# Perceiver attention scores: float32 keys and queries as 32-row tiles four abreast, in place of three products of rounded parts

## The reference, cut to what matters

```python
q = _qdq(x) @ _qdq(wq).T + bq
kv = cond @ wkv.T + bkv
k, v = jnp.split(kv, 2, axis=-1)          # 16 heads of width 16, 1601 keys
attn = jax.nn.softmax(jnp.einsum('bnhd,bmhd->bhnm', q, k) * scale, axis=-1)
o = jnp.einsum('bhnm,bmhd->bnhd', attn, v).reshape(B, N, C)
```

## Time and profile before

| | |
|---|---|
| median of 3 runs | 2300.67 us (2297.53 to 2301.21) |
| span of the profiled execution, first to last instruction | 2296.0 us |
| the rest of the median, outside of the span | 4.7 us |
| scores of the first strip, of the last | 33.4 us, 1759.8 us |
| TensorE matmul busy, mean granted clock | 2102.5 us (92%), 0.973 |
| VectorE busy, ScalarE busy, GpSimd busy | 1751.3 us (76%), 1441.0 us (63%), 684.0 us (30%) |

### The profile page before, as it was taken

How to read it: one execution, slowest core, us unless ns; L and a number is a source line. 1 busy time by engine, 2 the same in 40 slices (tenths; PEclk the granted TensorE clock), 3 DMA queues, 4 the chain that set the end, 5 groups by cost and what they waited for, 6 DMA issues and landing times. The chain is left out here.

```text
span 2296.0 us, 56054 instructions
## 1 busy us (share of the span) xinstructions
PE 2102.5 (92%) x21448; PEld 1456.2 (63%) x21448; DVE 1751.3 (76%) x3728; ACT 1441.0 (63%) x3012; POOL 684.0 (30%) x646
## 2 busy tenths in 40 slices
PE   7999999999999999999999999999997149999975
PEld 5666666666666666666666666666664037777754
DVE  5557887979797978888888888797978736656646
ACT  2667676768676767676777767676867124444433
POOL 1002040404131322213130404040403427767770
PEclk9999999999999999999999999999999569999998
DMA  7586672323132313232323323232310136676648
GB/s 226 192 288 210 235 250 75 114 82 89 72 89 72 93 70 91 77 83 79 100 88 82 97 64 105 55 105 68 107 47 25 56 119 212 199 229 209 201 138 331
DMA packets 132711, 294.16 MB, mean 128 GB/s; under 512 B 21899, under 2 KB 89143, under 8 KB 126304
## 3 DMA queue, kind: packets, MB, share of 16 engines
q1 hardware_dynamic: 114016, 255.89, 35.7%
q0 software_dynamic: 18432, 34.69, 4.3%
HBM read 165.40 MB, written 108.27 MB: 119 GB/s over the span
## 5 line engine op out<-in xcount | busy, mean ns | idle before, releaser
L801 ACT ACTIVATE sb_probs<-S,sb_negmax 128x1604 f32<-128x1604 f32 x256 | 409.2, 1598 | 278.5 <-DVE sb_negmax L979 277.0
L793 ACT ACTIVATE sb_probsT<-W 128x384 f32<-128x384 f32 (+1 forms) x1024 | 473.6, 513 | 68.2 <-PE W L639 65.3
L639 PE MATMUL W<-sb_ident,sb_probs 128*128 128x128 f32 (+1 forms) x3328 | 478.3, 280 | 15.7 <-DVE sb_o_tok L992 8.0
L979 DVE TENSOR_REDUCE sb_negmax<-S 128x1 f32<-128x1604 f32 x256 | 466.2, 1821 | 2.9 <-PE S L629 1.2
L639 PEld LDWEIGHTS W<-sb_ident,sb_probs 128*128 128x128 f32 (+1 forms) x3328 | 363.5, 139 | 133.9 <-issue 64.7
L612 PE MATMUL W<-sb_wkv_in,sb_ctx 128*128 128x256 f32 (+1 forms) x1664 | 410.7, 389 | 14.2 <-ACT sb_probsT L793 6.6
L602 PE MATMUL W<-sb_ctx,sb_wkv_in 128*32 128x401 f32 x4096 | 399.3, 504 | 4.4 <-DVE sb_V L973 2.9
L612 PEld LDWEIGHTS W<-sb_wkv_in,sb_ctx 128*128 128x128 f32 (+1 forms) x1664 | 293.3, 187 | 79.1 <-ACT sb_probsT L793 25.7
L1335 POOL DMA_INDIRECT y_scratch<-sb_ys,sb_places x256 | 264.4, 1033 | 112.1 <-issue 109.0
L963 DVE SCALAR_TENSOR_TENSOR sb_K_lo<-W,sb_pair_cols,sb_K_hi 128x401 fp32r<-128x401 f32 x256 | 162.2, 633 | 175.5 <-ACT sb_K_hi L785 175.2
L785 ACT ACTIVATE sb_K_hi<-W,sb_pair_cols 128x401 fp32r<-128x401 f32 x256 | 153.2, 598 | 181.5 <-PE W L602 181.4
(11 more groups left out here) (188 smaller groups left out, 2921.0 us busy)
## 6 DMA issues: line engine op xcount, KB each, us to landing
sb_ctx<-ctxT SPq DMA_DIRECT2D x32, 1604.0 KB, 7.7
xe_scratch<-sb_none SPq DMA_DIRECT2D x32, 1088.0 KB, 12.7
sb_xg<-xe_scratch SPq DMA_DIRECT2D x64, 544.0 KB
sb_BC<-bc_scratch SPq DMA_DIRECT2D x32, 1024.0 KB, 5.9
sb_Q_hi<-sb_q_hi SPq DMA_DIRECT2D x128, 128.0 KB, 4.5
sb_Q_lo<-sb_q_lo SPq DMA_DIRECT2D x128, 128.0 KB, 5.4
y_scratch<-sb_none SPq DMA_DIRECT2D x16, 1024.0 KB, 12.0
sb_rows<-y_scratch SPq DMA_DIRECT2D x16, 1024.0 KB, 8.1
```

What stands on the lines that cost most here:

```text
L639: ins = pe.transpose(W[0:keys_in(t), at * P:(at + 1) * P], probs[n % 2][:, t * P:t * P + keys_in(t)], ident[:])
L793: act.activation(probsT[k][n % (k + 1)][:, 0:wide], ring[bank_of("T", G, k)][:, 0:wide], ACT.Copy)\
L801: act.activation(probs[n % 2][:].rearrange("p (c k) -> p c k", c=QUADS), scores_of, ACT.Exp, bias=negmax[:, slot:slot + 1], accum_out=den[ ...
L979: dve.tensor_reduce(negmax[:, slot:slot + 1], scores_of, AX.XY, ALU.max, negate=True).then_inc(max_done, 1)
```

## The change

Keys and queries stay whole, in float32. ScalarE writes the keys once (`K`) and releases their bank; `k_low` is gone, and with it `K_lo`, `K_hi` and the semaphore between ScalarE and VectorE. GpSimd only places the queries (`q_own`), without the two further operations, and SyncE deals them with four DMAs for each half pair in place of eight. The scores are one product: four float32 matmuls, each on its own 32 rows of the array and into its own PSUM bank, in place of twelve matmuls of float32r.

```diff
 def freed_by(job):
-    return "act" if job[0] == "T" else "dve"
+    return "act" if job[0] in ("T", "K") else "dve"
...
-        K_hi, K_lo = (sb(f"K_{m}", [P, STRIPS, CK + 1], F32R) for m in ("hi", "lo"))
+        K = sb("K", [P, STRIPS, CK])
...
-        q_hi, q_lo = (sb(f"q_{m}", [P, STEPS, 2, N], F32R) for m in ("hi", "lo"))
-        Q_hi, Q_lo = ([sb(f"Q_{m}{n}", [P, STRIPS, 2, 2, N], F32R) for n in range(2)] for m in ("hi", "lo"))
+        Q = [sb(f"Q{n}", [P, STRIPS, 2, 2, N]) for n in range(2)]
...
-                for part, whole in ((q_hi, Q_hi), (q_lo, Q_lo)):
-                    for c in range(QUADS):
-                        sp.dma_start(whole[half][32 * c:32 * c + 32, :, :, :, :].rearrange("p s g h n -> p s (g h n)").bitcast(F32),
-                                     part[:, 2 * half:2 * half + 2, :, :].rearrange("p g h n -> p (g h n)").bitcast(F32)).then_inc(q_in[half], 16)
+                for c in range(QUADS):
+                    sp.dma_start(Q[half][32 * c:32 * c + 32, :, :, :, :].rearrange("p s g h n -> p s (g h n)"),
+                                 q_own[:, 2 * half:2 * half + 2, :, :].rearrange("p g h n -> p (g h n)")).then_inc(q_in[half], 16)
...
-                pool.tensor_tensor(q_own[:], *of_heads, ALU.mult).then_inc(q_own_up, 1)
-                pool.tensor_tensor(q_hi[:], *of_heads, ALU.mult).then_inc(q_hi_up, 1)
-                pool.wait_ge(q_own_up, i + 1)
-                pool.wait_ge(q_hi_up, i + 1)
-                pool.tensor_tensor(q_lo[:], q_own[:], q_hi[:].bitcast(F32), ALU.subtract).then_inc(q_up, 1)
+                pool.tensor_tensor(q_own[:], *of_heads, ALU.mult).then_inc(q_up, 1)
...
-                pe.wait_ge(ring_free["dve"], free_at("K", n))
+                pe.wait_ge(ring_free["act"], free_at("K", n))
...
-                products = ((Q_hi, K_hi), (Q_hi, K_lo), (Q_lo, K_hi))
-                for n, (q, k) in enumerate(products):
-                    for c in range(QUADS):
-                        rows = slice(32 * c, 32 * c + 32)
-                        cn = CK + 1 if c == 0 else CK - 1
-                        ins = pe.matmul(S[:, 512 * c:512 * c + cn], q[half][rows, s, g, :, :].rearrange("p h n -> p (h n)"),
-                                        k[rows, s, 0:cn], start=(n == 0), stop=(n == len(products) - 1))
+                for c in range(QUADS):
+                    rows = slice(32 * c, 32 * c + 32)
+                    cn = CK if c == 0 else CK - 1
+                    ins = pe.matmul(S[:, 512 * c:512 * c + cn], Q[half][rows, s, g, :, :].rearrange("p h n -> p (h n)"),
+                                    K[rows, s, 0:cn], start=True, stop=True)
...
-                act.activation(K_hi[:, s, 0:CK], ring[bank_of("K", n)][:, 0:CK], ACT.Identity,
-                               bias=pair_cols[:, g * STRIPS + s:g * STRIPS + s + 1]).then_inc(k_hi_up, 1)
+                act.activation(K[:, s, :], ring[bank_of("K", n)][:, 0:CK], ACT.Identity,
+                               bias=pair_cols[:, g * STRIPS + s:g * STRIPS + s + 1]).then_inc(ring_free["act"], 1)
...
-            def k_low(n):
-
-                _, g, s = step_of(n)
-                dve.wait_ge(k_hi_up, n + 1)
-                dve.scalar_tensor_tensor(K_lo[:, s, 0:CK], bank("K", n)[:, 0:CK],
-                                         pair_cols[:, g * STRIPS + s:g * STRIPS + s + 1],
-                                         K_hi[:, s, 0:CK].bitcast(F32), ALU.add, ALU.subtract).then_inc(ring_free["dve"], 1)
...
-                if G + STRIPS < ALL_STRIPS:
-                    k_low(G + STRIPS)
```

More of the change, by code:

```diff
@@ L321, in mixer_phase @@
         ring_free = {"act": sem("ring_free_act"), "dve": sem("ring_free_dve")}
-        k_hi_up = sem("k_hi_up")
         var_up = sem("var_up")
@@ L326, in mixer_phase @@
         q_f_up = sem("q_f_up")
-        q_own_up = sem("q_own_up")
-        q_hi_up = sem("q_hi_up")
         q_up = sem("q_up")
@@ L462, in _ @@
             pool.memset(neg_half[:], -0.5).then_inc(consts, 1)
-            for part in (K_hi, K_lo):
-                pool.memset(part[:, :, CK:CK + 1].bitcast(F32), 0.0).then_inc(consts, 1)
             pool.iota(iota_e[:], [[1, E]], base=0, channel_multiplier=0,
@@ L470, in _ @@
                       allow_small_or_imprecise_dtypes=True).then_inc(consts, 1)
-            pool.wait_ge(consts, 9)
+            pool.wait_ge(consts, 7)
             pool.affine_select(out=ident[:], in_=ident[:], compare_op=ALU.not_equal, fill=1.0, base=0,
@@ L478, in _ @@
                                pattern=[[1, P]], channel_multiplier=-1).then_inc(consts, 1)
-            pool.wait_ge(consts, 12)
+            pool.wait_ge(consts, 10)
             pool.affine_select(out=headmask[:], in_=headmask[:], compare_op=ALU.is_ge, fill=0.0, base=DH * STRIPS - 1,
                                pattern=[[DH * STRIPS, 2]], channel_multiplier=-1).then_inc(consts, 1)
-            pool.wait_ge(consts, 13)
+            pool.wait_ge(consts, 11)
             def rstd_q(i):
@@ L493, in part_q @@
                 for half in range(2):
-                    after(pool, q_in[half], 16 * 2 * QUADS * i)
+                    after(pool, q_in[half], 16 * QUADS * i)
                 of_heads = (q_f[:].rearrange("p b g n -> p (b g) n").unsqueeze(2).to_broadcast([P, STEPS, 2, N]),
                             headmask[:].unsqueeze(1).unsqueeze(3).to_broadcast([P, STEPS, 2, N]))
-                pool.tensor_tensor(q_own[:], *of_heads, ALU.mult).then_inc(q_own_up, 1)
-                pool.tensor_tensor(q_hi[:], *of_heads, ALU.mult).then_inc(q_hi_up, 1)
-                pool.wait_ge(q_own_up, i + 1)
-                pool.wait_ge(q_hi_up, i + 1)
-                pool.tensor_tensor(q_lo[:], q_own[:], q_hi[:].bitcast(F32), ALU.subtract).then_inc(q_up, 1)
+                pool.tensor_tensor(q_own[:], *of_heads, ALU.mult).then_inc(q_up, 1)
             def scan_input(p, unit):
@@ L564, in take @@
                 return ring[bank_of(*job)]
-            pe.wait_ge(consts, 13)
+            pe.wait_ge(consts, 11)
             def turn_w(rows, bank, parts):
@@ L619, in scores @@
                 if s == 0 and g == 0:
-                    pe.wait_ge(q_in[half], 16 * 2 * QUADS * (n // SLOTS + 1))
-                pe.wait_ge(ring_free["dve"], free_at("K", n))
+                    pe.wait_ge(q_in[half], 16 * QUADS * (n // SLOTS + 1))
+                pe.wait_ge(ring_free["act"], free_at("K", n))
                 after(pe, exp_done, n)
-                products = ((Q_hi, K_hi), (Q_hi, K_lo), (Q_lo, K_hi))
-                for n, (q, k) in enumerate(products):
-                    for c in range(QUADS):
-                        rows = slice(32 * c, 32 * c + 32)
-                        cn = CK + 1 if c == 0 else CK - 1
-                        ins = pe.matmul(S[:, 512 * c:512 * c + cn], q[half][rows, s, g, :, :].rearrange("p h n -> p (h n)"),
-                                        k[rows, s, 0:cn], start=(n == 0), stop=(n == len(products) - 1))
+                for c in range(QUADS):
[3 more added lines that the diff above has]
+                                    K[rows, s, 0:cn], start=True, stop=True)
                 ins.then_inc(s_done, 1)
@@ L1157, in _ @@
             for name, n in START:
-                if name == "K":
-                    k_low(n)
-                elif name == "XQ":
+                if name == "XQ":
                     x_up(0)
-                else:
+                if name == "Q":
                     q_out(0)
```

## The result

The changed kernel takes 2258.34 us (median of 4 runs, 2256.68 to 2259.12) against 2299.23 us for the kernel before on the same chip (4 runs): a ratio of 0.9813, 95% interval 0.9801 to 0.9826, or 41 us less. Forecast were 37 us less, 2264 us, with a range of 2238 to 2304.

What follows compares the result with a forecast made beforehand. TensorE's order of work was taken to bound the mixer, with some 80 us hanging on late VectorE. Scores +29, bank −21, VectorE's queue −45 gave −37 us, so 2264 us, range 2238 to 2304.

Steps and rivals of the forecast that it cites:

- The scores: TensorE's float32 scores: two groups of four abreast, 0.89 us for 0.75, 0.14 us more a strip, 29 us in all.
- Rivals two and three: Scores on TensorE: three says float32 row tiles don't run abreast, 2.04 us longer than forecast, 2786 us, chance 0.08.
- Rival two: Scores' second group on TensorE starts late: 0.33 us in 13 of 16 strips, 69 us for 29, 2304 us; chance 0.08.
- 13 of 16 strips pay: Share of the mixer's strips lengthened by the scores' extra 0.14 us on TensorE, 29 us together.
- rival four: Longer scores cost nothing on TensorE, since a wait follows them anyway: 2235 us; chance 0.04.
- Which strips don't pay: Three of each 16, where a small job precedes the values and their load waits for ScalarE's copy of the transposes.
- the forecast's 21 and 45: Gains from removing `k_low`: 21 us for the keys' bank freed earlier, 45 us for VectorE's queue (bounds 0 to 49.8).
- the term of 21 us for the bank: ScalarE instead of `k_low` releases the keys' bank, so TensorE's loads wait less: 21 us, bounds 17.9 to 29.6.
- What bounds the kernel: In the mixer TensorE's order of work sets the time, busy 389.59 of 400 us; some 80 us hang on late VectorE.
- the sum held: Whole kernel: 29 − 21 − 45 = −37 us, giving 2264 us.
- The query side: GpSimd's two dropped query operations and half of SyncE's dealing DMAs: not waited for, costed at nothing.
- Rival one: VectorE's waits stay, taken over by ScalarE's copies or matmul order: 2309 us with none of the 45; chance 0.14.

Runs made afterwards that it cites:

- the fourth corner: Kernel before without `k_low`: ScalarE releases the keys' bank, three float32r products stay, the second with rounded keys for their low part; 2232.84 us, ratio 0.9707.
- with `k_low` back: Changed kernel plus `k_low` in its old form, writing to a spare tile and releasing the keys' bank from VectorE; 2307.25 us, ratio 1.0034.
- with one product: Kernel before with only the first of its three float32r score products, `k_low` still made; 2295.28 us, ratio 0.9979.
- the ungated run: Kernel before with the split of the keys moved to GpSimd, without a later wait on the scores ahead of the copy; 2293.10 us, ratio 0.9973.
- the run with the narrow load: Changed kernel plus a one-source idle VectorE operation at `k_low`'s place, 690 columns, 230 in one strip of 16; 2296.74 us, ratio 0.9990.
- The idle operations with two sources: Changed kernel plus an idle two-source VectorE operation at `k_low`'s place, ScalarE still releasing the bank: 550 columns 2336.09 us, 401 columns 2310.69 us.
- the idle operations with one source: Changed kernel plus an idle `tensor_scalar` on VectorE at `k_low`'s place: 528 columns 2287.86 us; 690 columns, 230 in one strip, 2296.74 us.

## Why the prediction was right, step by step

*The scores.* Two groups of four abreast, 0.88 us for the forecast 0.89: the hand-overs of keys and of float32r scores, put together, give float32 row tiles. Rivals two and three (the tiles in turn) are out by the timeline. Rival two was that the second group starts only 0.19 us after the first has streamed: 0.33 us in 13 of 16 strips, 69 us in place of 29, and from it comes the upper end of the range, 2304 us. No run shows that delay; in the changed kernel the second group's loads run beside the first group's matmuls, through at 880.53, and its own matmuls start at 880.66. 13 of 16 strips pay, as forecast, 130 to 139 ns each. The cost on top of a kernel without `k_low` is 25.5 us for the forecast 29, so rival four (no cost) is wrong there; with `k_low` in place, at 8 us, it is nearly right. Which strips don't pay was partly right: of the four with a turned output 10 and 14 don't, but 2 and 4 do, and strip 0 is the third. In 10 and 14 the values' load waits for ScalarE's copy, as forecast, 0.68 us in the fourth corner and 0.55 with the longer scores.

*`k_low`.* Taken out with the scores as they were, it is worth 66 us: the sum of the forecast's 21 and 45. But the two terms are not what they were called. Without `k_low`'s length, holding the bank costs 1 us; with a load of about that length in the queue, the hold adds 11 to 12 us (2296.74 to 2307.25, and strips 9, 12 and 13). So the term of 21 us for the bank was mis-sized, as far as it was measured: a bank that comes back late is mostly the same lateness of VectorE, read off at another place. The queue is the rest. All this was run with the longer scores, where the two together are 49 us; how the 66 us split under the three products is open.

*What bounds the kernel.* This step failed in part. I wrote that TensorE's order of work sets the time, with 80 us hanging on VectorE. The runs with shorter and longer scores show that before, in 11 of 16 strips, the scores could take 0.38 or 0.88 us and the strip stayed as it was. What fits is a loop that goes past the scores: keys' matmuls, ScalarE's write, `k_low`, in most strips also the maximum and what follows it on VectorE, a bank read out by VectorE, TensorE's rest of the strip, keys' matmuls. Strip 2 of a pair with `k_low` back, the scores lying beside the write and `k_low`:

```profile
585.47 0.31 PEld L618 LDWEIGHTS S<-sb_K,sb_Q 32*128 32x128 f32 x8 [0.65 <-issue]
...
586.24 0.64 DVE L952 SCALAR_TENSOR_TENSOR sb_K_spare<-W,sb_pair_cols,sb_K 128x401 fp32r<-128x401 f32 x1 [1.82 <-ACT sb_K L774]
...
589.98 0.31 PEld L628 LDWEIGHTS W<-sb_ident,sb_probs 128*128 128x128 f32 x3 [0.53 <-DVE sb_o_tok L981]
```

The scores end at 586.42, `k_low` at 586.88, and VectorE then works without a pause up to the bank that TensorE waits for. If this sets the strip, the wait must shrink by what the scores gain and grow by what they lose. In this strip 0.66 us before become 0.53. In strip 13 the values' load waits 0.67 us before; with `k_low` back and with one product:

```profile
665.33 0.30 PEld L603 LDWEIGHTS W<-sb_wkv_in,sb_ctx 128*128 128x128 f32 x2 [0.52 <-DVE sb_K_spare L952]
```

```profile
984.98 0.30 PEld L612 LDWEIGHTS W<-sb_wkv_in,sb_ctx 128*128 128x128 f32 x2 [1.02 <-DVE sb_K_lo L963]
```

That is 0.15 us less for scores 0.13 us longer, and 0.35 more for scores 0.37 us shorter. In four pairs of the kernel before, each of the 11 strips has such a wait for VectorE, of 0.12 to 0.75 us; VectorE works without a pause up to it, in seven strips (2, 3, 5, 6, 10, 11, 12) since `k_low`, which waited for ScalarE, and in four (0, 1, 13, 14) since before it, in the scan. Strips 7, 8 and 15 have none. TensorE sets the time of most strips only once `k_low` is gone: there 0.50 us less a strip gives 96 us.

*Why the sum held.* In one order, first `k_low` out and then longer scores on top, the sums are right: 66 for 66, 25.5 for 29. In the other order they read 8 us for the scores and 49 for `k_low`. The difference of 17 us is where the longer scores lie in the shadow of VectorE's lateness. Had the change kept `k_low`, the same way of reckoning would have said 29 us for the scores and been wrong by 21. The prediction chose no order; it added its terms as if none depended on another, and 66 came out of two terms that were not confirmed singly. So that the sum came within 4 us is in part luck.

*The rest.* The query side costs nothing, as written. Rival one was wrong in the main: of 79.4 us of waits for VectorE (29.6 for the low part, 49.8 for the rest) 9.1 are left, while those of the values' load for ScalarE's copies rose from 25.7 to 38.3. (A row of 8.6 us on `sb_q_f` is, like the 132.7 us above, no wait: the load stands where it does in every strip, 0.88 us after the scores' first.) The waits on `sb_V` are not nearly gone, as was forecast: L685 keeps 4.8 of 10.9 us and L712 4.0 of 4.4. VectorE is busy 136 us less and not 162, as its rows overlap: before, the rows of `k_low` alone add 134 us to the busy time. In the timeline a row of 0.29 us of the scan starts at 988.53, so ends 0.08 us after `k_low` starts at 988.74.

## What to carry to other kernels

The busiest engine, at 97%, need not be the one that sets the time: make its suspected work shorter and see if the strip follows. When an edit adds work to one engine and takes it from another, cost the terms in a named order and measure the fourth corner, since each is worth what it is worth only with the other in place. An operation's price on a queue can be what stands behind it, more than the resource that it holds: here 37 to 38 us for the queue and 11 to 12 for the bank.

## What was not expected of the hardware

VectorE's and GpSimd's operations in SBUF took longer beside each other: in the ungated run above an addition took 1.15 us for 0.42, a cast 1.48 for 0.52. In the run with the narrow load VectorE's operation of 230 columns with one SBUF source starts beside GpSimd's operations on two SBUF sources and takes 1.37 us, as long as that of 528 columns did there (1.43 us), where 528 columns alone take 0.49 us:

```profile
844.72 1.37 DVE L953 TENSOR_SCALAR sb_K_spare<-sb_none,sb_pair_cols 128x230 f32<-128x230 f32 x1
```

```profile
844.67 3.77 POOL L503 TENSOR_TENSOR sb_bx<-sb_u,sb_BC 128x512 f32<-128x512 f32 x3 [14.52 <-DVE sb_u L1094]
```

Its length there hardly depends on its width, and it ends, at 846.09, 0.15 us after the first of GpSimd's operations (844.67 to 845.94), so it looks like waiting for that operation to end rather than like sharing. `k_low` itself, with one source in PSUM and one in SBUF, never showed this: all 256 took 626 to 640 ns, the one of this strip too, which in the kernel before stood beside the same operation of GpSimd (634 ns).

The idle operations with two sources show it too: that of 401 columns took 1.72 us where it starts together with GpSimd's. That of 550 columns was not held up (783 to 797 ns); there GpSimd's operation starts 0.16 us later and takes 1.76 us, for 1.27 in the median:

```profile
528.55 0.79 DVE L952 SCALAR_TENSOR_TENSOR sb_K_spare<-sb_none,sb_pair_cols 128x550 f32<-128x550 f32 x1
```

```profile
528.71 1.76 POOL L503 TENSOR_TENSOR sb_bx<-sb_u,sb_BC 128x512 f32<-128x512 f32 x1 [14.94 <-DVE sb_u L1094]
```

The idle operations with one source cost 84 ns for 162 columns more (495 ns for 528, 579 for 690), 0.52 ns a column; those with two cost 154 ns for 149 more (636 for 401, 790 for 550), 1.03. So a column cost the first, `tensor_scalar`, half as much. Why `k_low` was spared is not shown: unlike the load of 401 columns it has a source in PSUM, but no run here moved that source alone.
